# Seven block products for all four token chunks instead of two, in a fused feed-forward and convolution kernel

## The reference, cut to what matters

```python
xn = layernorm(x)                                   # x: 2048 tokens x 512
Wg, Wu, Wd = dequant_nf4(...)                       # 1792x512, 1792x512, 512x1792
h = silu(xn @ Wg.T) * (xn @ Wu.T)                   # 2048 x 1792
ffn = h @ Wd.T
conv = irfft(rfft(xn, 2L) * rfft(K, 2L))[:L] + D * xn   # K: S4 kernel, L = 512
out = x + conv + ffn
```

## Time and profile before

| | |
|---|---|
| median of 3 runs | 471.56 us (471.34 to 473.03) |
| the profiled execution | 473.78 us; its span from first to last instruction 472.0 us |
| busy over the span | PE 449.4 us (95%), DVE 376.8 (80%), ACT 275.3 (58%), POOL 182.7 (39%) |
| matmuls | 2598 |
| mean granted TensorE clock | 0.996 |

### The profile page before, as it was taken

One profiled execution on the slowest core, in us unless ns is written; L12 is line 12 of the kernel. 1 busy time (PEld: TensorE's weight loads), 2 busy tenths in 40 slices (PEclk: granted clock), 3 DMA queues, 4 the chain that ended last, 5 costly groups with the idle time before them and its releaser, 6 DMA issues.

```text
span 472.0 us, 7230 instructions
## 1 busy us (share of the span) xinstructions
PE 449.4 (95%) x2598; PEld 254.7 (54%) x2598; DVE 376.8 (80%) x605; ACT 275.3 (58%) x468; POOL 182.7 (39%) x181
## 2 busy tenths in 40 slices
PE   0789999999999999999999899999999999999997
PEld 0544444443444444444444344456544688888886
DVE  5879869987677687875886676864999899999993
ACT  8947565586767866567674865863332533544340
POOL 0552589503275653746557474666200000000000
PEclk9989999999999999999999999999999999999999
DMA  8372536112425234212231225235790021001111
GB/s 283 84 278 67 113 62 169 47 46 89 156 67 179 89 140 151 69 44 89 68 90 56 80 42 152 89 94 171 227 340 3 1 92 46 15 32 46 46 46 45
DMA packets 31832, 47.21 MB, mean 100 GB/s; under 512 B 13044, under 2 KB 14132, under 8 KB 31284
## 3 DMA queue, kind: packets, MB, share of 16 engines
q1 hardware_dynamic: 30516, 42.56, 29.3%
q0 software_dynamic: 1280, 4.20, 2.8%
HBM read 35.93 MB, written 8.72 MB: 95 GB/s over the span
## 4 chain that ended last, share of the span: by engine, by line
PE 65%; DVE 4%; DMA 4%; ACT 3%; issue 2%; POOL 2%; SPq 0%; DVEq 0%; POOLq 0%; ACTq 0%
PE bank L2196 20%; PE bank L1949 15%; PE bank L2090 15%; PE bank L2147 8%; PE bank L2137 6%; DMA lines<-wd 3%; POOL work L818 1%; ACT work L887 1%; ACT work L872 1%; DMA work<-in_q_down 1%; DVE work L1227 0%; DVE h L1348 0%; DVE work L1231 0%; DVE h L1291 0%; PE bank L2039 0%
## 5 line engine op out<-in xcount | busy, mean ns | idle before, releaser
L1949 PE MATMUL bank<-xT,w 128*128 128x512 f16 (+1 forms) x732 | 166.5, 380 | 1.9 <-DVE w L1241 1.7
L887 ACT ACTIVATE work<-work 128x512 f32<-128x512 int32 (+1 forms) x186 | 104.7, 621 | 36.7 <-POOL work L818 33.1
L1949 PEld LDWEIGHTS bank<-xT,w 128*128 128x128 f16 x732 | 72.3, 99 | 87.3 <-DVE w L1241 2.1
L818 POOL TENSOR_SCALAR work<-work 128x512 f32<-128x512 int32 x31 | 64.4, 2078 | 31.2 <-DVE work L1207 16.7
L2196 PE MATMUL bank<-wd,work 128*128 128x256 f16 x504 | 56.2, 273 | 0.0
L2196 PEld LDWEIGHTS bank<-wd,work 128*128 128x128 f16 (+1 forms) x504 | 49.3, 98 | 6.0
L831 POOL TENSOR_SCALAR w<-work,sc 128x512 f16<-128x512 f32 x17 | 28.3, 1664 | 55.3 <-DVE work L1231 55.2
L2090 PE MATMUL bank<-h 128*128 128x512 f16 x198 | 48.1, 379 | 1.5 <-DVE h L1291 1.5
L1167 ACT ACTIVATE work<-h 128x896 f16<-128x896 f32 x30 | 27.9, 943 | 28.4 <-DVE h L1857 18.3
L2196 PE MATMUL bank<-h,work 128*128 128x256 f16 x378 | 42.2, 273 | 0.0
L2196 PEld LDWEIGHTS bank<-h,work 128*128 128x128 f16 x378 | 37.0, 98 | 4.3
(11 more groups left out here) (192 smaller groups left out, 642.8 us busy)
## 6 DMA issues: line engine op xcount, KB each, us to landing
h<-in_x SPq DMA_DIRECT2D x8, 512.0 KB, 4.9
moved<-h SPq DMA_DIRECT2D x4, 1024.0 KB, 4.7
xT<-in_x POOLq DMA_DIRECT2D x16, 256.0 KB, 4.0
h<-moved SPq DMA_DIRECT2D x4, 1024.0 KB, 10.8
out<-xT SPq DMA_DIRECT2D x15, 256.0 KB, 2.1
work<-in_q_gate SPq DMA_DIRECT2D x14, 256.0 KB, 2.8
work<-in_q_up SPq DMA_DIRECT2D x14, 256.0 KB, 2.6
work<-in_am_gate SPq DMA_DIRECT2D x28, 128.0 KB, 3.0
```

What stands on the lines that cost most here:

```text
L818: pool.tensor_scalar(chain_room(u, "r"), qs[:, u % 2, :], RIGHT_FROM, RIGHT_FROM, ALU.max, ALU.subtract).then_inc(first_done, 1)
L887: nc.scalar.activation(room, qs[:, u % 2, :] if j == 0 else room, KNEE, scale=scale, bias=bias, alpha=below).then_inc(knee_done, 1)
L1949: mm = nc.tensor.matmul(out_b, weights(k)[:, unit, wl, f, :], xT[:, TPC * c + first:TPC * c + last, xl, f, :], start=(i == 0), stop=(i == ...
```

## The change

From tile 4 on, chunks 0 and 1 are also made by seven block products (side 1; chunks 2 and 3 are side 0). Six banks are used, a trio for each side. PE does each product number for side 0 and then side 1; product 4 of tile k moves into window k + 1. The token sums for side 1 are made once: `token_whole` by POOL, the rest by DVE and ACT in windows 3 and 4. `CHAINED` starts at unit 7 instead of 11, and POOL makes all high halves from there. The high half of chunk 0's h goes from ACT to POOL (`h_hi`). The small S4 steps of POOL move from ahead of its loop into it (`small_steps`). `EARLY_IN` has four windows instead of six. Six rows of h are moved to DRAM instead of four. The loads of the residual go from POOL's queue to SP's. The list of semaphores, the lines that only carry the side as an index, and the bodies of `exp_step` and `v_step` (the same 17 and 20 instructions as before, one for each i) are left out below.

```diff
-SILU_ORDER, H_ORDER = (0, 2, 1, 3), (0, 3, 1, 2)
-
-
-def in_order(chunks):
+ROLE_B, ROLE_E = (2, 0), (3, 1)
+FIRST_BLOCKED = (3, 4)
+A_BANK, E_BANK, B_BANK = (4, 0), (5, 1), (6, 2)
...
+SILU_SEQ = in_order((0, 2, 1, 3), (2, 0, 3, 1))
+H_SEQ = in_order((0, 3, 1, 2), (3, 1, 2, 0))
...
-EARLY_IN = (5, 6, 9, 10, 11, 12)
...
-DOWN_ROWS = (0, 1, 2, 3, 4, 12, 5, 6, 7, 8, 9, 10, 11, 13)
-CHAINED = range(11, UNITS)
-POOL_HALVES = range(CHAINED[0], UNITS - 4)
+DOWN_ROWS = tuple(range(NM))
+CHAINED = range(7, UNITS)
+POOL_HALVES = CHAINED
...
-            absmax_of(UNITS - 3)
             codes_of(UNITS - 2)
-            absmax_of(UNITS - 2)
-            codes_of(UNITS - 1)
-            absmax_of(UNITS - 1)
+            for t in range(NT):
+                load_residual(t)
+                if t == 2:
+                    codes_of(UNITS - 1)
+                for u in range(UNITS - 3, UNITS):
+                    if t == scaled_behind(u - 2) + 2:
+                        absmax_of(u)
...
+            def small_steps(u):
+
+                if made_before(3) <= u < made_before(4):
+                    for i in range(0, 9) if u == made_before(3) else range(9, EXP_STEPS):
+                        exp_step(i)
+                elif made_before(4) <= u < made_before(5):
+                    for i in range(0, 5) if u == made_before(4) else range(5, 10):
+                        v_step(i)
+                elif u in (made_before(7), made_before(7) + 1):
+                    for i in range(10, 15) if u == made_before(7) else range(15, V_STEPS):
+                        v_step(i)
+                    if u == made_before(7) + 1:
+                        pool.wait_ge(v_done, V_STEPS)
+
+            def token_whole(i):
+
+                c, f = ((1, 0), (0, 0), (1, 2), (0, 2))[i]
+                if i == 0:
+                    pool.wait_ge(xlo_done, TURNED)
+                    for j in range(2):
+                        pool.wait_ge(xt_ld[j], 16 * TPC)
+                hi, lo = (xT[:, TPC * c:TPC * c + TPC, l, f:f + 2, :] for l in (HI, LO))
+                pool.tensor_tensor(x_sums[1][i].rearrange("p (f t m) -> p t f m", f=2, t=TPC), hi, lo,
+                                   ALU.add).then_inc(xb_done[1], 1)
+
+            def h_hi(k):
+
+                pool.wait_ge(h_done, H_COUNT[NCH * k])
+                pool.tensor_copy(hs[:, HOME[k], HI, :], sil[:, 0, :]).then_inc(hhp_done, 1)
...
+                    if LAST_USE[before] is not None:
                         pool.wait_ge((gate_done, up_done)[unit % 2], WHOLE_COUNT[LAST_USE[before]])
+                    for s in sides(before):
+                        pool.wait_ge(m_done[s], m_at(s, before, (2, 4)[unit % 2]))
...
-            pool.wait_ge(v_done, V_STEPS)
             first_pass(CHAINED[0])
+            first_pass(CHAINED[1])
+            for i in range(4):
+                token_whole(i)
             for u in POOL_HALVES:
-                first_pass(u + 1)
+                if CHAINED[1] < u + 1 < UNITS:
+                    first_pass(u + 1)
+                for k in range(4, NM):
+                    if u == (made_before(k + 1) if k < NM - 1 else TAIL - 1):
+                        h_hi(k)
+                if u == UNITS - 1:
+                    pool.wait_ge(conv_done, NT)
                 weight_hi(u)
                 gate_copy(u)
+                small_steps(u)
                 if u == made_before(NM - 3) - 1:
                     turned_rows()
-            first_pass(UNITS - 3)
-            first_pass(UNITS - 2)
-
-            for t in range(NT):
-                pool.wait_ge(conv_done, t + 1)
-                pool.dma_start(res[:, t, :], x_v[:, t, :]).then_inc(xr_ld[t], 16)
-                if t == 3:
-                    first_pass(UNITS - 1)
...
+            def part(k, first, last):
+                items(eighths(ACT_AT, k, first), eighths(ACT_AT, k, last))
+
+            def first_window(k):
+                n = NCH * k
+                silu(n)
+                items(ACT_AT[9] - 3, ACT_AT[9])
+                copy_m1(0, k)
+                h_hi(n)
+                copy_m5(0, k)
+                part(k, 0, 2)
+                token_hi(1, 0)
+                part(k, 2, 3)
+                silu(n + 2)
+                part(k, 3, 5)
+                silu(n + 1)
+                token_hi(1, 1)
+                part(k, 5, 6)
+                silu(n + 3)
+                part(k, 6, 8)
+                block_hi(k + 1, 0)
+                block_hi(k + 1, 1)
+                token_hi(1, 2)
+                token_hi(1, 3)
+
             def window(k):
                 n = NCH * k
-                if k == NM - MOVED:
-                    act.wait_ge(moved_st, 16 * MOVED)
-
-                def part(first, last):
-                    items(eighths(ACT_AT, k, first), eighths(ACT_AT, k, last))
-
+                if HOME[k] != k:
+                    act.wait_ge(moved_st[HOME[k]], 16)
+                part(k, 0, 3)
+                copy_m1(0, k)
+                part(k, 3, 4)
+                copy_m1(1, k)
+                copy_m5(0, k)
+                copy_m5(1, k)
+                part(k, 4, 6)
+                silu(n + 2)
                 silu(n)
-                copy_m1(k)
-                if k > BLOCKED[0]:
-                    part(0, 2)
-                h_hi(n)
-                copy_m5(k)
-                if k == BLOCKED[0]:
-                    items(ACT_AT[9] - 3, ACT_AT[9])
-                    part(0, 2)
-                part(2, 3)
-                silu(n + 2)
-                part(3, 5)
+                part(k, 6, 7)
+                silu(n + 3)
+                part(k, 7, 8)
                 silu(n + 1)
-                part(5, 6)
-                silu(n + 3)
-                part(6, 8)
-                block_hi_of(k + 1, 0)
-                block_hi_of(k + 1, 1)
-
-            def block_hi_of(k, part):
-                if k in BLOCKED:
-                    block_hi(k, part)
-
-            for k in range(3, NM):
+                if k + 1 < NM:
+                    block_hi(k + 1, 0)
+                    block_hi(k + 1, 1)
+
+            first_window(3)
+            for k in range(4, NM):
                 window(k)
-            items(ACT_AT[made_before(NM - 1) + LAST_UNITS], ACT_AT[UNITS])
-            weight_hi(UNITS - 1)
+            items(ACT_AT[TAIL - 1], ACT_AT[UNITS])
...
+                if is_blocked(n):
+                    dve.wait_ge(hhp_done, k - FIRST_BLOCKED[1] + 1)
+                    made = sil[:, 0, :]
+                else:
+                    dve.wait_ge(hhi_done, LO_COUNT[n])
+                    made = bank[2 * pair_of(n) + 1][:]
+                v.tensor_tensor(hs[:, HOME[k], LO, CH * c:CH * c + CH].bitcast(BF16), made,
...
+            def first_window(k):
+
                 def part(first, last):
                     items(eighths(DVE_AT, k, first), eighths(DVE_AT, k, last))
 
+                n = NCH * k
+                part(0, 2)
+                token_sum(1, 0)
+                h_mul(n)
+                token_sum(1, 1)
+                h_lo(n)
+                part(2, 4)
+                join(0, k, 0)
+                token_sum(1, 2)
+                part(4, 6)
+                token_sum(1, 3)
+                part(6, 8)
+                other_sums(k + 1)
+                block_lo(k + 1, 0)
+                token_lo(1, 0)
+
+            def window(k, stage=None):
                 def stage_of(first, last):
                     for slot in range(first, last):
-                        part(slot, slot + 1)
+                        items(eighths(DVE_AT, k, slot), eighths(DVE_AT, k, slot + 1))
                         if stage:
                             stage(slot)
 
-                n = NCH * k
-                if k == NM - MOVED:
-                    dve.wait_ge(moved_st, 16 * MOVED)
-                if k == BLOCKED[0]:
+                n, both = NCH * (k - 1), k > FIRST_BLOCKED[1]
+                join(0, k - 1, 1)
+                h_mul(n + 3)
+                if both:
+                    join(1, k - 1, 1)
+                h_mul(n + 1)
+                block_lo(k, 1)
+                if not both:
+                    token_lo(1, 1)
+                h_mul(n + 2)
+                stage_of(0, 2)
+                if both:
                     h_mul(n)
+                stage_of(2, 5)
+                if both:
                     h_lo(n)
-                    stage_of(0, 2)
-                    join(k, 0)
-                    stage_of(2, 4)
-                else:
-                    stage_of(0, 2)
-                    h_mul(n)
-                    stage_of(2, 3)
-                    h_lo(n)
-                    stage_of(3, 4)
-                    join(k, 0)
...
-            for k in range(3, NM - 7):
+                else:
+                    token_lo(1, 2)
+                    token_lo(1, 3)
+                join(0, k, 0)
+                stage_of(5, 6)
+                join(1, k, 0)
+                stage_of(6, 8)
+                if k + 1 < NM:
```

(99 more changed lines are left out.)

404 lines of the change are left out of this document (222 added, 182 removed).

## The result

The changed kernel takes **526.44 us** (median of 4 runs, 525.31 to 529.17) against 471.56 (471.34 to 473.03) of the kernel before: ratio 1.1165, 95% interval 1.1116 to 1.1214. Predicted were 497 us and 475 to 510. The sign was right; the time lies 29 us above the forecast and 16 above the range.

The account below looks back on a forecast made before the run. PE was taken as the bound, busy 217.60 of 221.26 us in the windows. New gaps of 42.0 us less 16.6 saved gave +25.4 us on 473.78, put 2.2 lower for the median: 497 us, range 475 to 510.

Parts of the forecast that it names:

- The sign: Whole kernel: the change was forecast to make it slower, +25.4 us, with chance 0.84 for slower.
- The ring in three-unit windows: Windows 5, 6, 9, 12, 13: product 6 of side 1 waits through ACT, POOL and DVE on product 4; 23.4 us.
- Small steps: POOL's exponential and V steps, now ahead of first passes, delay windows 3, 4 and 7; 10.1 and 2.3 us.
- turned_rows: Window 11: on POOL it stands ahead of b's first pass and delays product 6; 5.0 us, at least 3.
- Window 3, 1.2 us ahead of `copy_m1`: Three passes ahead of `copy_m1` in window 3, moved by the longer chain, leave a 1.2 us gap, at least 0.
- the clock: Rival: PE's clock falls after long gaps, 1.4 us at each of eight, 508 us; over 505 (or longer chain) 0.11.
- The rule named in that rival: Skill page on TensorE: half rate is the default and activity releases it, so the clock would fall at long gaps.
- `token_whole` "hidden up to 4" us: POOL's four token sums of 1024 elements, 1.5 to 4 us each, costed at nothing.
- The rule that the prediction weighed and set aside: Two-input DVE and SBUF-reading GpSimd instructions fully exclude each other; would hold `h_hi` 0.6 us per ring, 3 in all.
- my 0.4 us: Loss read from the earlier trace for a DVE step beside a POOL pass, 1.07 instead of 0.68 us.
- the residual, "some 5 us in hand": Residual loads on SP behind three pairs of absmax loads; DVE needs the first 13 us into the convolution; costed at nothing.
- "From the convolution on, the same 161 us": Convolution to end of kernel: time expected unchanged at 161 us.

Follow-up runs that it names:

- e1: Changed kernel with ACT doing both sides' copies of product 1 ahead of l0 and r0 of the third unit in three-unit windows; 510.93 us.
- e2: Changed kernel with POOL's small S4 steps spread over units 9 to 24 and put ahead of the high half; 522.24 us.
- e3: Changed kernel with POOL's `turned_rows` moved from ahead of the next first pass to behind it; 524.57 us.
- e6: Changed kernel with 14 unused matmuls ahead of product 6 of side 1 in windows 5, 6, 9, 12 and 13; 523.02 us.
- e7: Changed kernel with POOL's four token sums of side 1 replaced by fills with zero; 523.34 us.
- e9: On top of the four edits, DVE instead of POOL makes the whole-token sums of side 1, inside window 3; 484.30 us.
- e4: Changed kernel with the first residual loads on SP's queue put ahead of the codes of the last two units; 519.85 us.
- e10: e9 with DVE's joins moved ahead of steps that wait for POOL in three-unit windows, second joins also in window 3; 475.74 us.
- e12: e10 with window 3 rewritten: DVE's first join ahead of side 1's token work, ACT's first token high half two passes later; 478.53 us.
- the four edits: Changed kernel with ACT's copies first, small steps spread, `turned_rows` behind a first pass and residual loads ahead of codes; together 487.97 us.

## Why the prediction was wrong in its number

**The ring in three-unit windows: right in mechanism, and in the sum of its sizes.** Predicted 23.4 us; measured 5.88, 5.01, 5.45, 4.43 and 4.30, 25.1 us. e1 removes all five. The sum is closer than its parts, which is luck: window 9 was given 4.1 us, with nothing added, and has 5.45; windows 12 and 13 were given over 5 each, for codes that queue on SP, and have 4.4 and 4.3. `h_hi` took 1.22 us in the mean (1.3 taken), but 1.60 in windows 5, 6 and 9 and 1.00 in 12 and 13, and the first pass of b in window 5 took 2.49 (2.0 taken).

**Small steps: right in place, too dear.** 10.1 + 2.3 us predicted; windows 4 and 5 have 6.79 + 0.58 + 0.24, window 8 0.64. The nine steps took 5.4 us (6.5 taken), and e2, which moves them, leaves 2.60 of the 6.79, so not all of it is shown to be theirs. **turned_rows:** 5.0 predicted, 4.53 measured, and e3 removes it. **Window 3, 1.2 us ahead of `copy_m1`:** 1.09 measured. In all, 42.0 us of gaps were forecast in the windows and 44.6 measured, of which 5.7 are no part of the forecast.

**First step that failed: the clock was a rival and not a term (+20 us).** The prediction gave it 1.4 us at each of eight gaps and little chance, since no gap of 4 to 8 us in dense work was in the rows. Measured are 16.1 us in the windows and 4.0 behind them. In the windows the rival's price was near: the eight long gaps cost 1.2 to 2.5 us each, 14.2 in all, where it had 8 x 1.4 = 11.2. In window 5 it was 1.28 us on product 6 and 1.21 on the twelve matmuls behind it. What failed was to leave it out: e6 shows that it is the idle time that does it, and with 42 us of gaps already in the sum, the clock belonged in it. The rule named in that rival, from the Trainium skill, page TensorE: Matmul & The Clock Gate, Part 1, is that activity releases the full clock. e6 agrees with it: with its matmuls of no use in the gaps the full clock stayed in four windows of five.

**Second: `token_whole` "hidden up to 4" us (+5.7 us with the 0.29 behind it, less 3.0 by which the other gaps were over-sized).** The duration of 2.77 us was within bounds, and the step still failed: it asked how long POOL would be busy and not what DVE does beside it. e7 and e9 show it. The rule that the prediction weighed and set aside in favour of a row (the Trainium skill, SBUF — State Buffer, Who interferes with whom) is nearer to these rows than my 0.4 us: one SCALED was held by 1.9 us. I had applied it to `h_hi` only, where it would have added 3 us, and not to the one edit that puts long instructions on POOL. The earlier trace rows remains true, 1.07 instead of 0.68 us beside a pass, so the hold is not equally long for every POOL instruction; what sets its length the runs don't settle.

**Third: the residual, "some 5 us in hand" (+7.9 us of gaps).** I counted the absmax loads on SP (an absmax is a weight block's scale), and not the loads of the last two units' codes, which wait for POOL's first pass, which waits for DVE, which waits for the residual. "From the convolution on, the same 161 us" was wrong by 11.9 (7.7 + 4.1 + 0.1). e4 removes the gaps. The queue was named; what its head waits for wasn't followed to the end.

**The sum closed.** The forecast was +25.4 us on the span. 25.4 + 20.1 (clock) + 7.9 (residual) + 5.7 - 3.0 (gaps in the windows) - 3.0 (the opening, a chance of the two profiled executions) gives the measured +53.1. The 60 matmuls fewer and their 12.95 us were right.

**What the change is worth in itself.** With the orders of e10 it takes 475.74 us. The 12.95 us of matmuls are used up by DVE's token work in window 3 (4.35 us of gap and 1.3 us of slow matmuls), and by the 7.5 us of gaps from window 5 on. e12 speaks for a lack of room and not of order in the first. Whether DVE could be relieved of it in the opening wasn't tried. There POOL stood idle for 11.10 us, waiting for codes, just ahead of a first pass and the sums; putting the sums first wasn't tried either. So it stays open whether the change could ever pay here.

## What to carry to other kernels

When work is taken from the bound engine, follow what its waits now stand behind on every other engine, and through each queue until the loop closes or ends: two of the large losses here, 25.1 and 7.9 us of gaps, were rings, of engines with idle time to spare. Where a sum holds gaps of several microseconds ahead of dense matmuls, put the clock into it as a term. And an instruction given to an idle POOL can have a second price, the two-input steps of DVE beside it. Last, compare runs by their ratio to one kernel measured beside them: by bare medians the four edits seemed worth 10 us more together than one by one.

## What the runs showed of the hardware

Gaps of 4.3 to 6.8 us in dense work were followed by matmuls at 1.2 GHz: 2.74 instead of 1.46 us for six, and 2.75 to 4.03 for the next twelve, 1.2 to 2.5 us lost for each gap. In e6, with 3.19 us of matmuls of no use inside the gap and 1.4 to 2.4 us of idle behind them, the full clock stayed in four windows; with 2.86 us it fell. In other runs some gaps of 2.1 to 2.4 us were followed by slow matmuls and some were not.

DVE steps with two inputs from SBUF took 1.95 and 2.62 us (0.74 and 0.69 alone) beside POOL sums of 2.77 us, and 1.29 and 1.52 beside POOL copies of 1.48 us. An `h_mul` that takes one of its inputs from a bank took 0.74 us beside such a sum (77.62), as it did alone. POOL pays as well: `weight_hi(7)`, beside DVE's token steps, took 3.60 us instead of 1.57.
